# Shared expert's products started beside the layer norms, in a gated cross-attention and mixture-of-experts kernel

## What is computed

```python
def _L0_xattn_ref(x, adj, W, b):
    si = jnp.einsum('bnd,d->bn', x, Wi[0])
    sj = jnp.einsum('bnd,d->bn', x, Wj[0])
    xij = jax.nn.sigmoid(si[:, :, None] + sj[:, None, :] + b[0])
    return P_ASEM * xij + (1.0 - P_ASEM) * adj
...
    x = x + jnp.tanh(g_xattn[0]) * _L0_xattn_ref(ctx_512, _layernorm(x, axis=-1), L0_xattn_W, L0_xattn_b)
    x = x + jnp.tanh(g_ffn[0]) * _L0_ffn_ref(_layernorm(x, axis=-1), ...)
```

## Time and profile before

| | |
|---|---|
| median of 3 runs | 719.21 us (718.24 to 724.73) |
| profiled execution | 718.56 us, its span 716.5 us |
| mean granted TensorE clock | 0.939 of full speed |
| TensorE busy in the span | 88% |
| VectorE busy | 71% |
| ScalarE, POOL busy | 44%, 45% |

### The profile page before, as it was taken

How to read it: one execution, slowest core, us unless ns; L and a number is a source line. 1 busy time by engine, 2 the same in 40 slices (tenths; PEclk the granted TensorE clock), 3 DMA queues, 4 the chain that set the end, 5 groups by cost and what they waited for, 6 DMA issues and landing times.

```text
span 716.5 us, 17273 instructions
## 1 busy us (share of the span) xinstructions
PE 626.9 (88%) x4394; PEld 381.9 (53%) x4395; DVE 509.0 (71%) x1297; ACT 313.3 (44%) x542; POOL 320.1 (45%) x505
## 2 busy tenths in 40 slices
PE   4112769999999799999999999999999999999991
PEld 3112445665556456656556566565565555566550
DVE  5999768936668586768888868588678888867110
ACT  2324483122335255455445454454554544554541
POOL 1454620000013465555465475564655546565532
PEclk9655679999999899999999999999999999999997
DMA  7661235102116668584886876758576786754432
GB/s 231 208 199 42 78 104 136 64 1 89 59 31 190 161 151 196 102 203 86 186 174 134 191 161 149 172 110 195 120 185 131 154 205 115 179 89 88 82 45 37
DMA packets 48523, 93.72 MB, mean 131 GB/s; under 512 B 7677, under 2 KB 15339, under 8 KB 48498
## 3 DMA queue, kind: packets, MB, share of 16 engines
q0 software_dynamic: 16128, 38.35, 28.6%
q1 hardware_dynamic: 32370, 55.07, 27.0%
HBM read 65.16 MB, written 28.24 MB: 130 GB/s over the span
## 4 chain that ended last, share of the span: by engine, by line
PE 69%; DVE 15%; issue 4%; ACT 3%; DMA 3%; POOL 2%; DVEq 2%; SPq 2%; POOLq 0%; ACTq 0%
PE gu_ps L1116 41%; PE bank L1143 19%; PE bank L1155 4%; PE bank L1130 4%; DVE stats L683 2%; DMA dn_sc<-dn_scale_halves 2%; DVE wgu L875 1%; PE bank L1169 1%; DVE act L942 1%; ACT acth L575 1%; POOL mix_room L415 1%; ACT xT L544 1%; DVE wdn L881 1%; DVE dq_mag L860 1%; DVEq L942 1%
## 5 line engine op out<-in xcount | busy, mean ns | idle before, releaser
L1116 PE MATMUL gu_ps<-wgu,mix_room 128*128 x1728 | 306.3, 327 | 1.7 <-DVE tick L898 1.3
L1116 PEld LDWEIGHTS gu_ps<-wgu,mix_room 128*128 128x128 f16 x1728 | 166.5, 98 | 114.1 <-issue 8.0
L1143 PE MATMUL bank<-wdn,aT 128*128 (+1 forms) x792 | 185.4, 379 | 1.0 <-ACT aT L582 1.0
L582 ACT ACTIVATE aT<-bank 128x768 f16<-128x768 f16 x88 | 71.3, 810 | 150.4 <-PE bank L1130 150.4
L494 POOL DMA_INDIRECT out<-mix_room,idx_s x72 | 120.0, 1667 | 17.5 <-issue 17.5
L1143 PEld LDWEIGHTS bank<-wdn,aT 128*128 128x128 f16 x792 | 77.5, 98 | 85.3 <-issue 1.6
L471 POOL COPY idx_g<-room_b 128x1 int32 (+1 forms) x72 | 60.6, 841 | 112.8 <-DVE tick L816 61.8
L942 DVE SCALAR_TENSOR_TENSOR act<-gu_ps,wslot,sg x72 | 44.5, 618 | 88.1 <-ACT sg L568 77.5
L491 POOL COPY idx_s<-room_b 128x1 int32 (+1 forms) x72 | 19.2, 267 | 186.2 <-DMA out<-mix_room,idx_s 105.5
L575 ACT ACTIVATE acth<-act 128x384 f16<-128x384 f32 x88 | 46.0, 523 | 119.8 <-DVE act L942 119.8
L474 POOL DMA_INDIRECT room_b<-token_rows,idx_g x72 | 75.4, 1047 | 11.0 <-issue 1.4
(11 more groups left out here) (161 smaller groups left out, 632.6 us busy)
## 6 DMA issues: line engine op xcount, KB each, us to landing
dn_sc<-dn_scale_halves SPq DMA_DIRECT2D x34, 384.0 KB
dn_raw<-in_L_ffn_down_packed SPq DMA_DIRECT2D x48, 256.0 KB
gu_sc<-gu_scale_halves SPq DMA_DIRECT2D x34, 192.0 KB
X<-in_x SPq DMA_DIRECT2D x4, 1024.0 KB, 10.8
token_rows<-room_a SPq DMA_DIRECT2D x16, 256.0 KB, 2.0
out<-X SPq DMA_DIRECT2D x4, 1024.0 KB, 4.4
gu_raw<-in_L_ffn_gate_up_packed SPq DMA_DIRECT2D x16, 192.0 KB
gu_raw<-in_L_ffn_gate_up_packed SPq DMA_DIRECT2D x16, 191.9 KB
```

The lines of the kernel that those rows point to most:

```text
L582: nc.scalar.activation(aT[:, b].rearrange("p a c t -> p (a c t)"), at_ps, ACT.Copy).then_inc(aT_done, 1)
L1116: mm = nc.tensor.matmul(ps[b][:, 0:I], x(xp * HC + c), wgu[:, w, wp, c, col:col + I], start=(c == 0 and xp == 0 and wp == 0), stop=(c == H ...
L1143: mm = nc.tensor.matmul(y_ps[b][:, :], aT[:, b, ap, t, :], wdn[:, w, wp, t, :], start=(n == 0), stop=(n == 3 * IC - 1))
```

## The change

- The scales are loaded and split as one block of 128 rows by 612. `ctx_512` and `X` are issued from ScalarE's queue, `X` once the scales are there. The shared expert's scales are stored and loaded ahead of the others', its packed words are loaded before the wait for that store.
- `sig` gets a place for all 16 tiles, in the room of `xT` (the transposed rows); `scaled_x` works in place in `X`. The scores are made batch by batch, the row scores too (`row_scores(b)`), and no longer wait for `attend`. `attend` and the second statistics are separate calls.
- `normalised` is gone: ScalarE makes the high half and the float row `xn` from `X` (two operations with a scale and a bias, `high_x`), POOL the low half (`low_x`).
- Only the tiles of batch 0 are transposed ahead of the shared products. All four gate-up parts of the shared weights are unpacked first, then slots 0 and 1 start; the four down parts come after. `attend(1)` and the second statistics of batch 1 follow. First statistics of batches 2 and 3 come in slot 2, `attend(2)` in slot 3, `attend(3)` in slot 4. Rows 4 to 15 are transposed in slots 3 to 8 (`WITH_X`), two in each; there is one PSUM bank for them.
- The work of `after_shared_slot` moves: expert 0's weights to slots 5 to 8, `route` to slot 9, `ranks`, `tables` and `positions` to 10, `token_weights` (the second half of `route`) and `mark(0)`, `mark(1)` to 11, `mark(2)`, `mark(3)` to 12, `lists` to 13.
- `values` is laid out tile by tile, the slots innermost (before: the 16 tiles innermost).
- `dequant` shifts the word by `4 * g` in its first two operations; the seventh operation, which shifted `gu_half` in place, is gone.
- `down` of all shared slots uses one PSUM bank and waits for the `add_y` of the slot before.

The core of the diff (left out: the declarations, the split's new shapes, helpers that only moved):

```diff
-        sig, xmix, xn = (mix_room[:, k] for k in range(3))
+        spare, xmix, xn = (mix_room[:, k] for k in range(3))
+        sig = xT[:, :].rearrange("p i a c t -> p i (a c t)").bitcast(F32)
...
         values = mix_room[:, 1:3].rearrange("p k b h -> p (k b h)").bitcast(F16)[:, 0:2 * SLOTS * NT]\
-            .rearrange("p (b s i) -> p b s i", b=2, i=NT)
-        place = sig.rearrange("p b h -> p (b h)").bitcast(F16).rearrange("p (q i) -> p q i", i=NT)
-        slot_room = wdn[:, 1].rearrange("p a c n -> p (a c n)")
...
+            for k, ap in enumerate((sh_gu_scales.rearrange("g n -> (g n)"), gu_scales.rearrange("e g n -> (e g n)"),
+                                    sh_dn_scales.rearrange("g n -> (g n)"), dn_scales.rearrange("e g n -> (e g n)"))):
+                sp.dma_start(sc_all[:, columns(k)], spread(ap, k)).then_inc(ld_sc, 16)
...
             sp.wait_ge(vs, SPLIT_STEPS)
...
+            for part, done in ((0, st_sc_sh), (1, st_sc)):
+                for k, dram in ((part, gu_s_dram), (2 + part, dn_s_dram)):
+                    for hl in range(2):
+                        flat = dram[hl, part:1 + part * E].rearrange("e g n -> (e g n)")
+                        sp.dma_start(spread(flat, k), sc_h[:, hl, columns(k)]).then_inc(done, 16)
+                if part == 0:
+                    load_words(sp, sh_gu_packed, sh_dn_packed, 0)
+            sp.wait_ge(st_sc_sh, 64)
+            load_scales(sp, 0, 0)
+            load_words(sp, gu_packed[0], dn_packed[0], 1)
             sp.wait_ge(st_sc, 64)
-            load_expert(sp, sh_gu_packed, sh_dn_packed, 0, 0)
-            load_expert(sp, gu_packed[0], dn_packed[0], 1, 1)
+            load_scales(sp, 1, 1)
...
-                    nc.gpsimd.tensor_scalar(xmix[:, i % 2, :], X[:, i, :], lnA[:, i:i + 1], lnB[:, i:i + 1],
+                    nc.gpsimd.tensor_scalar(X[:, i, :], X[:, i, :], lnA[:, i:i + 1], lnB[:, i:i + 1],
...
+                nc.gpsimd.tensor_tensor(xhl[:, i % ROWS_AHEAD, 1, :], xn[:, i % 2, :], xhl[:, i % ROWS_AHEAD, 0, :],
+                                        ALU.subtract).then_inc(xl_ready, 1)
...
             inverse_std(0, 0)
+            scaled_x(0)
             inverse_std(0, 1)
-            scaled_x(0)
+            scaled_x(1)
+            inverse_std(1, 0)
+            norm_factors(0)
+            low_halves_x(0)
+            inverse_std(1, 1)
+            norm_factors(1)
             inverse_std(0, 2)
-            scaled_x(1)
             inverse_std(0, 3)
-            for b in range(B - 1):
-                inverse_std(1, b)
-                normalised(b)
-                if b + 2 < B:
-                    scaled_x(b + 2)
-            inverse_std(1, B - 1)
-            normalised(B - 1)
-            pool.wait_ge(x1_ready, NT)
+            low_halves_x(1)
+            scaled_x(2)
+            inverse_std(1, 2)
+            norm_factors(2)
+            scaled_x(3)
+            low_halves_x(2)
+            inverse_std(1, 3)
+            norm_factors(3)
+            low_halves_x(3)
...
+            for b in range(B):
+                load_ctx(b)
+            a.wait_ge(ld_sc, 64)
+            for b in range(B):
+                load_x(b)
...
+            def scores(b):
+                a.wait_ge(sj_ready, b + 1)
+                a.wait_ge(si_ready, b + 1)
+                for i in range(b * TB, (b + 1) * TB):
+                    nc.scalar.activation(sig[:, i, :], sj_ps[b][:, :], ACT.Sigmoid,
+                                         bias=si[:, i:i + 1]).then_inc(sig_ready, 1)
+            def high_x(i):
+                a.wait_ge(xs2_ready, 3 * (i // TB) + 3)
+                if i >= ROWS_AHEAD:
+                    a.wait_ge(xT_ps_ready, i - ROWS_AHEAD + 1)
+                    a.wait_ge(st_rows[i % ROWS_AHEAD], 16 * (i // ROWS_AHEAD))
+                nc.scalar.activation(xhl[:, i % ROWS_AHEAD, 0, :], X[:, i, :], ACT.Identity, scale=xs2[:, i:i + 1],
+                                     bias=xm2[:, i:i + 1]).then_inc(xh_ready, 1)
+                if i >= 2:
+                    a.wait_ge(xl_ready, i - 1)
+                nc.scalar.activation(xn[:, i % 2, :], X[:, i, :], ACT.Identity, scale=xs2[:, i:i + 1],
+                                     bias=xm2[:, i:i + 1]).then_inc(xn_ready, 1)
...
-            halves(B - 1)
-            copy_xT(NT - 2)
-            copy_xT(NT - 1)
+            scores(2)
+            scores(3)
+            for i in range(TB):
+                high_x(i)
+                if i:
+                    copy_xT(i - 1)
+            copy_xT(TB - 1)
...
-            a.wait_ge(lg_ps_ready, NT)
-            nc.scalar.activation(lgh[:, :, :], lg_ps[:, :].rearrange("p (t k e) -> p t k e", k=2, e=E)[:, :, 1, :],
-                                 ACT.Copy).then_inc(lgh_ready, 1)
             copy_aT(0, 0)
-            a.wait_ge(lsub_ready, 1)
-            nc.scalar.activation(r_exp[:, :, :], lg[:, :, :], ACT.Exp).then_inc(exp_ready, 1)
             for i in range(2, NT):
                 copy_aT(i - 1, (i - 1) % 2)
+                if i in WITH_X:
+                    copy_xT(2 * i - 2)
+                if i == 11:
+                    a.wait_ge(lsub_ready, 1)
+                    nc.scalar.activation(r_exp[:, :, :], lg[:, :, :], ACT.Exp).then_inc(exp_ready, 1)
                 if i == NT - 1:
                     take_rows(0, 0)
                 activate(i, i % 2)
+                if i in WITH_X:
+                    copy_xT(2 * i - 1)
+                if i == 2:
+                    for k in range(TB, 2 * TB):
+                        high_x(k)
+                if i in WITH_X and 2 * i + 2 < NT:
+                    high_x(2 * i + 2)
+                    high_x(2 * i + 3)
+                if i == 9:
+                    a.wait_ge(lg_ps_ready, NT)
+                    nc.scalar.activation(lgh[:, :, :], lg_ps[:, :].rearrange("p (t k e) -> p t k e", k=2, e=E)[:, :, 1, :],
+                                         ACT.Copy).then_inc(lgh_ready, 1)
...
-                    link(nc.vector.tensor_scalar(dq_sign[:, :], gu_half[:, :], 0x8000, None, ALU.bitwise_and), wait=False)
-                    link(nc.vector.tensor_scalar(dq_mag[:, :], gu_half[:, :], 3, 0x0E00, ALU.logical_shift_right,
-                                                 ALU.bitwise_and), wait=d is None)
+                    if g == 0:
+                        link(nc.vector.tensor_scalar(dq_sign[:, :], gu_half[:, :], 0x8000, None, ALU.bitwise_and), wait=False)
+                        link(nc.vector.tensor_scalar(dq_mag[:, :], gu_half[:, :], 3, 0x0E00, ALU.logical_shift_right,
+                                                     ALU.bitwise_and), wait=d is None)
+                    else:
+                        link(nc.vector.tensor_scalar(dq_sign[:, :], gu_half[:, :], 4 * g, 0x8000, ALU.logical_shift_left,
+                                                     ALU.bitwise_and), wait=False)
+                        link(nc.vector.tensor_scalar(dq_mag[:, :], gu_half[:, :], 4 * g - 3, 0x0E00, ALU.logical_shift_left,
+                                                     ALU.bitwise_and), wait=d is None)
...
-                    link(nc.vector.tensor_scalar(gu_half[:, :], gu_half[:, :], 4, None, ALU.logical_shift_left), wait=False)
...
+            x_factors(0)
             first_stats(1)
-            v.wait_ge(si_ps_ready, 1)
-            nc.vector.tensor_scalar(si[:, :], si_ps[:, 0:NT], bias[:, 0:1], None, ALU.add).then_inc(si_ready, 1)
-            x_factors(0)
-            first_stats(2)
+            row_scores(1)
+            x_factors(1)
             attend(0)
-            x_factors(1)
-            first_stats(3)
-            attend(1)
-            x_factors(2)
-            x_factors(3)
+            row_scores(2)
+            second_stats(0)
+            row_scores(3)
             take_words(0, 0)
             for k in range(PARTS):
-                if k == 2:
-                    attend(2)
-                dequant(0, 0, k, k - 1 if k else None, fill=lambda: low_x(2 * k))
-                low_x(2 * k + 1)
-            end_gate_up(0, 0)
-            attend(3)
-            low_halves_x(2)
-            low_halves_x(B - 1)
-            dequant(0, 0, None, PARTS - 1)
-            end_dequant(0)
+                dequant(0, 0, k, None)
+            v.wait_ge(dqs, 1 + PARTS * G_STEPS)
+            nc.vector.memset(tick[:, 0:1], 0.0).then_inc(dqg_ready, 1)
...
-                                             place[:, 0:SLOTS, :], ALU.is_equal))
-                nc.vector.tensor_tensor(values[:, j % 2], values[:, j % 2], token1[:, :].unsqueeze(1).broadcast_to(by_slot),
+                by_slot = [P, NT, SLOTS]
+                step(nc.vector.tensor_tensor(values[:, j % 2], pos_slot[:, j, :].unsqueeze(2).broadcast_to(by_slot),
+                                             slot_h[:, :].unsqueeze(1).broadcast_to(by_slot), ALU.is_equal))
+                nc.vector.tensor_tensor(values[:, j % 2], values[:, j % 2], token1[:, :].unsqueeze(2).broadcast_to(by_slot),
```

(94 more changed lines are left out.)

225 lines of the change are left out of this document (107 added, 118 removed).

## The result

The changed kernel takes 755.17 us (median of 4 runs, 753.83 to 758.26) against 719.81 (4 runs, 718.24 to 724.73): ratio 1.0478, 95% interval 1.0439 to 1.0516. I had said 715 with a range of 705 to 729. The profiled execution has a span of 752.1 us.

The account below looks back on a forecast made before the run. VectorE sets the pace up to 77.7 us, TensorE after. Slot 0's start 44 plus stretch 159 gives 203 against 206.2, 3.2 us earlier; with -0.5 behind, 718.56 - 3.7 = 714.9, said 715, range 705 to 729.

Parts of the forecast that it names:

- the last of the sum: Behind `down(14)`: one operation less per unpacked part, `add_y(15)` ahead of `down(16)` about 0.5 us; together -0.5 us.
- The rule of mine: Sign of being wrong: the part behind `down(14)`, 510 us long, changes by more than 3 us.
- D: Start of slot 0, set by VectorE's chain: 44 us, bounds 41 to 50, 33.7 us earlier than before.
- S: Stretch from the start of slot 0 to the end of `down(14)`: 159 us, against 128.5 before.
- the 30 us given back: Of slot 0's 34 us gain: waits of slots 3 and 4 20, marks 6, transposes and routing inside slots 8.
- the second rival: Shared weights come late because X shares the DMA engines: slot 0 starts at 50, total 722 us; chance 0.18.
- The contention allowed for: Before slot 0, POOL's four low halves meet VectorE's gate-up parts and both lose time: 2 us added.
- Slots 3 and 4: TensorE idles 9.3 us for POOL's low half, then 6.6 us for ScalarE's copy; half clock returns.
- Marks: Slots 12 to 14: operations over `values` take 1.49 us, not 0.82; a mark 4.1 us in place of 2.75.
- GpSimd's low half: The two-input low-half operation on POOL takes an estimated 1.2 us; no row showed it.
- The slower rival: POOL's low half takes 3.7 us and sets the pace: 730 us; over 1% slower from 3.1 us; chance 0.15.
- One operation less: Dropping one operation per unpacked part is off TensorE's path behind `down(14)`, except where `activations` is late.

Follow-up runs that it names:

- 40 memsets: The changed kernel with 40 one-column memsets, unused by the result, ahead of VectorE's first wait: 716.02 us, 0.9921 of the kernel before.
- 89 and 104 memsets: 89 memsets ahead of VectorE's first wait in the kernel before: 758.1 us; 104 memsets ahead in the changed kernel: 756.14 us, one run.

## Why the prediction was wrong

**The step that failed is the last of the sum**: "Behind it one operation less per unpacked part is off TensorE's path ... Together -0.5". I took the 510 us behind `down(14)` as they were because no instruction there changed for the worse. The runs show that they cost 509 where VectorE's loop lies well and 545 where it lies badly, and that 54 instructions less ahead of it moved it from the one to the other. In kernels that differ in nothing but memsets this decides over 37 to 63 us. No rival of mine held it. A count of the instructions ahead of the loop, which I had not made, would have shown the move, though not its price. The rule of mine that a change of over 3 us behind `down(14)` would prove me wrong has done its work.

**With the loop in its place the total is nearly the forecast's**: 716.0 measured, 715 said. That is luck in part, since the terms erred both ways: D came 8 us late, S was 4 short, the part behind `down(14)` 1 short (508.6, said 509.8), and the median happens to lie 1.3 below the profiled execution (717.34), which alone is 2.4 above my sum. The parts that I named for the 30 us given back also add up to 34 (20, 6 and 8). Term by term, in the changed kernel:

- *D*: 51.8, said 44 (bounds 41 to 50). VectorE was done with the second statistics and row scores at 31.4, where I had 31.3 with the word copy; then it waited 6.2 us for the shared weights. This is the second rival, given 0.18, and it happened a little beyond its D = 50; its total of 722 did not come with it, since S was shorter. The contention allowed for is there: beside GpSimd's low halves one operation of 0.56 us took 1.46, a pair of 1.03 took 1.99 and the word copy 1.20 for 0.56, 2.5 together, where I had added 2. VectorE's two equal operations and the low half, in the changed kernel's timeline:

```profile
43.09 1.15 POOL L448 TENSOR_TENSOR room_a<-mix_room,room_a 128x512 f16<-128x512 f32 x1 [1.01 <-ACT mix_room L571]
```
```profile
43.19 1.46 DVE L903 TENSOR_TENSOR dq_mag<-dq_mag,dq_sign 128x768 uint16<-128x768 uint16 x1
...
46.80 0.56 DVE L903 TENSOR_TENSOR dq_mag<-dq_mag,dq_sign 128x768 uint16<-128x768 uint16 x1
```

- *S*: 155.1, said 159. Slots 3 and 4, from 76.3 to 111.3, took 35.0 where D+26.1 to D+61.1 is also 35.0; the idle times are 9.67 and 7.02, said 9.3 and 6.6, with the releasers named, and the half clock came back both times (3.72 and 4.02 us where 2.11 is full clock). Slots 5 to 8 took 7.47 each, said 7.65. The 4 us lie elsewhere: slots 0 to 2 ended at D+24.5, said D+26.1, and slot 13 with its lists at D+139.0, said D+142.2.
- *Marks*: 1.49 us per operation over `values`, as taken from the slot table (four of 1.484 and four of 1.491). The rule of the Trainium skill that I weighed (VectorE: DVE Perf Modes, "What auto-detection actually checks") agrees. What I mis-sized is the other side: the list matmuls fell from 5.05 per 32 to 1.19 per 16, which I had given nothing. The new layout costs 2 us net at `down(14)`, not 6, and nothing that the medians show.
- *GpSimd's low half*: 1.15 to 1.30 us, 1.16 in the median, said 1.2. The slower rival needed 3.1.
- *One operation less*, taken as next to nothing behind `down(14)`: with 1.2 us counted in D, it is worth some 4 us in all.

**What was right in mechanism and still misleading**: the waits of slots 3 and 4 are where I put them, but I read the queue orders as their cause. Sorted queues gained nothing (716.05); moving ten us of VectorE's statistics out, with GpSimd's queue sorted to follow, gained 13. So the order alone was not the bound, and VectorE's work behind it was at least part of it. Moving the statistics without touching GpSimd's queue was not run.

## What to carry to other kernels

- Where an engine's program has a loop with branches, an edit anywhere ahead of it moves it. Count the instructions ahead of the loop and in it, before and after, those that only wait for a semaphore too, and look at the page's row of instruction packets: if it grows with the number of turns, the loop is being refetched. A pad in idle time is a cheap test, and here a cure.
- Judge an edit that shortens a program by more than one placement. The six-step unpacking alone reads as 8.6% slower, and is worth 0.6% faster.
- A wait named by its releaser is a place, not a size: before changing an order, find what is second in line.

## What the runs showed of the hardware

- A loop of 322 or 334 instructions on VectorE ran without fetching (14 or 15 instruction packets in the whole execution) or fetched five pieces of 8 KB per turn (39 to 41). Which of the two it was follows in all eleven kernels from whether the loop touches three or four pieces of 128. The Trainium skill (Runtime: NRT & Kernel Launch, "Instruction fetch mechanics") gives two lines of 256 instructions; 89 and 104 memsets, which two such lines would bear, cost 37 and 40 us. The measurement decides: pieces of 128 here.
- VectorE then stood still for 5.2 to 8.7 us at each branch back, and for 11.0 to 12.8 where the loop began at most 8 instructions ahead of a piece's edge (by the second count); without fetching the wait at the first branch back was 0.9 us (the kernel before) and 1.25 (40 memsets).
- An fp16 comparison or product over 1280 elements took 0.82 us with both inputs moving in the innermost dimension and 1.49 with one repeated there.
- Sixteen matmuls with 80 moving columns took 1.14 to 1.19 us with the columns side by side and 2.53 with a column every 32 bytes (5.06 us per 32).
- VectorE's 16-bit operations over 768 elements took 0.6 to 1.0 us longer where one of GpSimd's two-input operations ran beside them: a copy 1.20 for 0.56, a pair of products 1.99 for 1.03, an operation of two inputs 1.46 for 0.56.
